# Attention steps taken in pairs in a two-stage vision block on one Trainium2 core

## The chip, the core and the metric

The kernel runs on one core of a Trainium2 chip. The metric is the device time of one execution in microseconds; for the kernel before it is 3094.75 us, the median of three runs. Times in the text are microseconds unless marked ns.

## What is computed

For each of 4 images of 32 x 32 tokens with 384 channels a selective scan comes first and attention second, both with a residual. The change touches the attention alone. Cut to that:

```python
qkv = (x.reshape(B, L, dim) @ w_qkv + b_qkv).reshape(B, L, 3, nh, hd)   # L = 1024, nh = 12, hd = 32
...
q = rot(q)
k = rot(k)
attn = jnp.einsum('bnqd,bnkd->bnqk', q, k) * scale
...
attn = attn.reshape(B, nh, H, W, H, W) + rel_h[..., :, None] + rel_w[..., None, :]
attn = jax.nn.softmax(attn.reshape(B, nh, L, L), axis=-1)
out = jnp.einsum('bnqk,bnkd->bnqd', attn, v)
out = out.transpose(0, 2, 1, 3).reshape(B, H, W, dim)
return out @ w_proj + b_proj
```

## The kernel before

The scan stage takes the first 1.7 ms and is not touched. Then each image has its attention by itself, some 347 us each. An image begins with a start phase (projections of q and k, values, relative-position tables; `START`) and then runs 96 steps: 3 groups of 4 heads (`GROUPS`, `HG`), 8 blocks of 128 queries in a group (`QB`), one head in a step. In step s = 32 g + k, the block is k // 4 and the head k % 4.

A step has these parts. TensorE's `scores(s)` (L880) multiplies one block's queries by all 1024 keys: two products of 64 rows of the array, one in its upper and one in its lower half, with the relative bias folded in as further rows. VectorE's `biased_scores(s)` (L1201) adds the bias of the other axis, writes the result to a buffer `PR` in SBUF and takes the negated maximum. ScalarE (L1526) takes the exponential in place and the row sum. TensorE's `turn_probs(s)` (L891) transposes the 128 x 1024 probabilities in eight pieces of the full array. `save_turned(s)` copies them from PSUM to `PT`: VectorE (L1155) for even s, ScalarE (L1503) for odd s. After a block's four steps, `weigh` (L905) multiplies by the values, 64 products of 32 columns of the array each, in two halves of 32; ScalarE's `save_sums` (L1509) copies the result.

PSUM has eight banks. A step's scores and its transposes take two banks each out of banks 0 to 5, so three places turn; bank 6 holds the weighing, bank 7 the jobs. Jobs are work of the next group that is put between the steps: a projection in two steps of a group (`proj`, six matmuls, L561; ScalarE's copy L1495; VectorE's two products L1125 and L1126; GpSimd's sum L1636) and the relative tables (`rel` L854 and L1141, `relh` L843 and L1146), at the steps of `JOB_AT`. Each job's output has bank 7, so its matmuls wait until the job before was copied out. In the last group `LATE` puts the sums' transposes (L925), the normalisation (L934, then L1171 and L1172 on VectorE) and half of the output projection (L561, L1179) in the same way; each waits for the one before.

The order is that of the loops in each engine's program. TensorE issues `scores(s + 2)`, then the job, then half a weighing in every second step, then `turn_probs(s)`. At a change of group SyncE loads 4 heads' operands with 6 DMAs each (L542), as soon as the last scores of the old group with that head are done, that is after step 28 + j of the group for head j; `scores` of the first four steps of a group wait for them. An image ends with `invert_sums(2)` (L1189), the last sums' transposes, weighing 23 and the rest of the projection (L948). The next image's start phase follows at once.

## Time and profile before

| | |
|---|---|
| median of 3 runs | 3094.75 us (3092.77 to 3095.74) |
| profiled execution | 3094.16 us, span 3092.4 us |
| busy share of the span | TensorE 87%, VectorE 73%, ScalarE 52%, GpSimd 44% |
| first scores of images 0 to 3, from the span's start | 1737.13, 2083.66, 2429.98, 2777.37 us |
| mean granted TensorE clock | 0.968 of full; 1.00 in the attention after its first start phase |

The profile has a timeline of each engine (start and duration, and in brackets how long the engine had been idle and what released it), groups of instructions by line, and windows with the busy time of each engine in a stretch. The ends of matmuls are modelled, and neighbours overlap: the time that a block of matmuls takes from the engine is read from its start to the start of the next block. The first and the last attention image of the trace run alike, so that image 1 stands for all four here.

### The profile page before, as it was taken

The page shows a single profiled execution, that of the slowest core. Times are in us where ns is not written, and L with a number is a line of the kernel's source. Part 1 is how long each engine was busy: PE and PEld are TensorE (multiplying, and loading weights), DVE is VectorE, ACT ScalarE, POOL GpSimd, SP SyncE. Part 2 cuts the span into 40 slices and gives each one's busy share as a digit, 9 for nine tenths or more (in the row PEclk, how much of TensorE's full clock was granted, in tenths as well). Part 3 has the DMA queues.
Part 4 walks back from the last instruction along what each step waited for, and adds up shares of the span by engine and source line. Part 5 has one row for each costly group of instructions (what it writes and reads, how often), then busy time and mean ns, then how long its engine had stood idle before and what let it go on. Part 6 is the DMA issues. An engine that isn't in the chain of part 4 may idle for free. (4 is left out here: it accounts for less than half of the span.)

```text
span 3092.4 us, 40835 instructions
## 1 busy us (share of the span) xinstructions
PE 2684.6 (87%) x16088; PEld 1346.6 (44%) x16088; DVE 2242.5 (73%) x2157; ACT 1614.7 (52%) x1972; POOL 1351.2 (44%) x624
## 2 busy tenths in 40 slices
PE   5579788988889878687767999999999999999999
PEld 2134233333333333232322565555555565556555
DVE  0398988899888998899992566646665566646665
ACT  2464655555555556555541456625564356525564
POOL 1577887887778877788670200011000300011000
PEclk9799999999999999999996999999999999999999
DMA  2344544455444555445551210120120210120110
GB/s 78 108 142 129 163 150 144 150 140 168 165 145 148 142 170 167 154 160 140 197 172 36 76 36 18 39 75 1 36 56 14 63 36 22 35 76 1 35 36 22
DMA packets 93526, 297.03 MB, mean 96 GB/s; under 512 B 16172, under 2 KB 18872, under 8 KB 93208
## 3 DMA queue, kind: packets, MB, share of 16 engines
q1 hardware_dynamic: 93336, 294.43, 30.8%
q8 instruction: 128, 2.10, 0.3%
q14 instruction: 62, 0.51, 0.1%
HBM read 238.27 MB, written 23.07 MB: 85 GB/s over the span
## 5 line engine op out<-in xcount | busy, mean ns | idle before, releaser
L1599 POOL TENSOR_TENSOR arena<-arena 128x1024 f32<-128x1024 f32 x384 | 903.2, 2357 | 307.4 <-DVE arena L1081 297.7
L1081 DVE TENSOR_TENSOR_SCAN arena<-PS,arena 128x1024 f32<-128x1024 f32 x384 | 879.0, 2289 | 102.2 <-ACT PS L1442 70.9
L577 PE MATMUL PS<-arena,ident 128*128 128x512 f32 x1536 | 762.0, 620 | 15.0 <-ACT arena L1453 12.8
L1442 ACT ACTIVATE PS<-arena,a_inf,a_neg 128x1024 f32<-128x1024 f32 x384 | 463.8, 1208 | 586.3 <-DVE arena L1081 580.3
L1201 DVE CUSTOM_DVE_ANT_1 arena<-PS,arena 128x1024 f32<-128x1024 f32 x384 | 467.7, 1219 | 323.4 <-PE PS L880 321.8
L1526 ACT ACTIVATE arena<-arena,neg_max 128x1024 f32<-128x1024 f32 x384 | 441.0, 1148 | 494.8 <-DVE neg_max L1201 494.8
L1089 DVE TENSOR_TENSOR arena<-arena,PS 128x1024 f32<-128x1024 f32 x384 | 460.8, 1200 | 57.7 <-PE PS L568 56.4
L568 PE MATMUL PS<-arena,sel 96*128 96x512 bf16 x768 | 239.4, 394 | 295.5 <-DVE arena L1089 291.7
L1629 POOL TENSOR_TENSOR arena<-arena 128x512 f32<-128x512 f32 x48 | 68.4, 1425 | 955.2 <-ACT arena L1495 955.2
L880 PE MATMUL PS<-arena 64*128 64x512 f32 x1536 | 431.6, 640 | 19.3 <-DMA arena<-arena 12.8
L577 PEld LDWEIGHTS PS<-arena,ident 128*128 128x128 f32 x1536 | 302.5, 198 | 275.0 <-issue 221.4
L891 PE MATMUL PS<-ident,arena 128*128 128x128 f32 x3072 | 414.7, 278 | 3.8 <-ACT arena L1526 3.6
L891 PEld LDWEIGHTS PS<-ident,arena 128*128 128x128 f32 x3072 | 334.9, 142 | 154.9 <-issue 92.5
L568 PEld LDWEIGHTS PS<-arena,sel 96*128 96x128 bf16 x768 | 55.9, 100 | 577.5 <-DVE arena L1089 503.3
L1155 DVE COPY arena<-PS 128x1024 f32<-128x1024 f32 x192 | 233.9, 1218 | 60.6 <-PE PS L891 57.2
L905 PEld LDWEIGHTS PS<-arena 128*32 128x32 f32 x6144 | 157.0, 110 | 134.0 <-issue 131.7
L905 PE MATMUL PS<-arena 128*32 128x128 f32 x6144 | 206.5, 276 | 0.0
L1503 ACT ACTIVATE arena<-PS 128x1024 f32<-128x1024 f32 x192 | 192.7, 1004 | 19.4 <-PE PS L891 19.4
L880 PEld LDWEIGHTS PS<-arena 64*128 64x128 f32 x1536 | 116.5, 185 | 88.5 <-issue 59.0
L1636 POOL TENSOR_TENSOR arena<-arena 128x512 f32<-128x512 f32 x48 | 64.0, 1333 | 176.3 <-DVE arena L1126 175.7
L561 PE MATMUL PS<-normed,arena 128*128 128x512 f32 x288 | 135.7, 615 | 0.6 <-DVE g_tmp L1025 0.6
L577 PE MATMUL PS<-arena 128*128 128x512 f32 (+1 forms) x224 | 108.3, 622 | 12.0 <-ACT arena L1305 5.5
(125 smaller groups left out, 2205.3 us busy)
## 6 DMA issues: line engine op xcount, KB each, us to landing
arena<-b_rows SPq DMA_DIRECT2D x256, 512.0 KB, 3.7
arena<-b_rows SPq DMA_DIRECT2D x256, 256.0 KB, 3.9
arena<-arena SPq DMA_DIRECT2D x192, 128.0 KB, 3.3
arena<-arena SPq DMA_DIRECT2D x120, 64.0 KB, 2.6
normed<-x_in SPq DMA_DIRECT2D x12, 512.0 KB, 5.4
residual<-x_in SPq DMA_DIRECT2D x12, 512.0 KB, 5.6
x<-residual SPq DMA_DIRECT2D x12, 512.0 KB, 5.3
xn<-residual SPq DMA_DIRECT2D x12, 512.0 KB, 4.7
```

What stands on the lines that cost most here:

```text
L568: last = pe.matmul(dst[:, half(h)], lhs, rhs(h), start=(k == 0), stop=(k == len(pairs) - 1))
L577: last = pe.matmul(dst[:, half(h)], lhs, rhs[:, half(h)], start=start, stop=stop, skip_group_check=True)
L880: last = pe.matmul(scores_place(s)[:, h * HALF:(h + 1) * HALF], QX[rows, j, qb * P:(qb + 1) * P], KX[rows, j, :], start=True, stop=True)
L891: last = pe.transpose(turned_place(s)[:, t * P:(t + 1) * P], PR[s % 3][:, t * P:(t + 1) * P], idn)
L905: last = pe.matmul(banks(6, 1)[HD * j:HD * j + HD, (n % 2) * P:(n % 2 + 1) * P], V[:, t, head * HD:(head + 1) * HD], PT[:, n % 2, j, t, :] ...
L1081: dve.tensor_tensor_scan(HS[:, at % 2, ::step], DA[:, ::step], DBU[:, at % R3, ::step], 0.0, ALU.mult, ALU.add).then_inc(scan_done.sem, 1)
L1089: dve.tensor_tensor(HC[:, at % R_HC, :], HS[:, at % 2, :], C_PSUM, ALU.mult).then_inc(hc_ready.sem, 1)
L1155: dve.tensor_copy(PT[:, n % 2, s % HG, :, :], turned_place(s).rearrange("p (t q) -> p t q", t=QB)).then_inc(pt_saved[0].sem, 1)
L1201: dve.tensor_tensor_reduce(out=PR[s % 3].rearrange("p (h w) -> p h w", w=IMG), in0=scores_place(s).rearrange("p (h w) -> p h w", w=IMG), i ...
L1442: act.activation(DA, DELTA[:, tile % 2, :], ACT.Exp, bias=a_inf[:, col:col + 1], scale=a_neg[:, col:col + 1]).then_inc(da_ready.sem, 1)
L1526: act.activation(PR[s % 3], PR[s % 3], ACT.Exp, bias=neg_max[:, s % 4:s % 4 + 1], scale=-1.0, accum_out=row_sum[:, qb, at:at + 1]).then_in ...
L1599: pool.tensor_tensor(DBU[:, at % R3, :], DU[:, tile % 2, :], BSB[:, at % R3, :], ALU.mult).then_inc(dbu_ready.sem, 1)
```

## The change

Steps go in pairs (s even, s + 1). TensorE issues `scores(s + 2)` and `scores(s + 3)`, the pair's job, a whole weighing of 64 products when s is a multiple of 4, then `turn_probs(s)` and `turn_probs(s + 1)`. A fourth `PR` buffer lies in `group_mean`, which is not used in this stage. The scores of a step and its transposes now have the same place (`step_place`), and a place is shared by steps 1 and 2, 3 and 4 and so on. So `scores(s + 2)` waits until VectorE has read step s + 1 (`max_done`), and `turn_probs(s + 1)` until it has read step s + 2. VectorE takes both steps of a pair, then copies the odd step's transposes out, then does its share of the jobs; ScalarE copies the even step's. The jobs of group 0 stand at steps 2, 4, ..., 28.

```diff
-        PR = [from_mats(k)[:, 0, :] for k in (6, 7, 26)]
+        PR = [from_mats(k)[:, 0, :] for k in (6, 7, 26)] + [
+            W["group_mean"][:, :, :].rearrange("p k c -> p (k c)")[:, 0:L]]
...
-        def step_banks(n):
-            return banks((0, 4, 2)[n % 3])
-        def scores_place(s):
-            return step_banks(s if s < 3 else 2 * s - 2)
-        def turned_place(s):
-            return step_banks(2 * s + 3)
+        def step_place(s):
+            return banks((4, 0, 2)[(s + 1) // 2 % 3])
...
-        JOB_AT = [{k: m for m, k in enumerate([2, 4, 6, 8, 10, 12, 16, 18, 20, 22, 24, 25, 26, 27])}, {6: 0, 10: 1}, {}]
+        JOB_AT = [{2 + 2 * m: m for m in range(len(JOBS[1]))}, {6: 0, 10: 1}, {}]
...
-                    if s == 1:
+                    if s == 0:
                         pe.wait_ge(rel_saved.sem, rel_saved.after(b, 2))
-                    elif s == 3:
-                        pe.wait_ge(max_done.sem, max_done.after(b, 2))
-                    elif s >= 4:
-                        wait_turned_saved(s - 4)
+                    elif s % 2 == 0:
+                        pe.wait_ge(max_done.sem, max_done.after(b, s))
+                    elif s >= 5:
+                        wait_turned_saved(s - 5)
                     for h in range(2):
                         rows = slice(2 * HD * h, 2 * HD * h + 2 * HD)
-                        last = pe.matmul(scores_place(s)[:, h * HALF:(h + 1) * HALF],
+                        last = pe.matmul(step_place(s)[:, h * HALF:(h + 1) * HALF],
                                          QX[rows, j, qb * P:(qb + 1) * P], KX[rows, j, :], start=True, stop=True)
                     last.then_inc(s_psum.sem, 1)
                 def turn_probs(s):
                     pe.wait_ge(exp_done.sem, exp_done.after(b, s + 1))
-                    if s + 1 < STEPS * GROUPS:
+                    if s % 2 and s + 1 < STEPS * GROUPS:
                         pe.wait_ge(max_done.sem, max_done.after(b, s + 2))
-                    else:
-                        wait_turned_saved(s - 3)
+                    elif s % 2 == 0 and s:
+                        wait_turned_saved(s - 1)
                     for t in range(QB):
-                        last = pe.transpose(turned_place(s)[:, t * P:(t + 1) * P], PR[s % 3][:, t * P:(t + 1) * P], idn)
+                        last = pe.transpose(step_place(s)[:, t * P:(t + 1) * P], PR[s % 4][:, t * P:(t + 1) * P], idn)
                     last.then_inc(pt_psum.sem, 1)
...
                 scores(0)
                 scores(1)
-                for s in range(STEPS * GROUPS):
+                for s in range(0, STEPS * GROUPS, 2):
                     g, k = divmod(s, STEPS)
                     if s + 2 < STEPS * GROUPS:
                         scores(s + 2)
-                    if k in JOB_AT[g]:
-                        job(g + 1, JOB_AT[g][k])
-                    if g + 1 == GROUPS and k in LATE_AT:
-                        late(LATE_AT[k])
-                    if s % 2 == 1 and s > HG:
-                        weigh((s - HG - 1) // HG, (s - HG - 1) % HG // 2)
-                    if s + 1 == STEPS * GROUPS:
+                        scores(s + 3)
+                    for k in (k, k + 1):
+                        if k in JOB_AT[g]:
+                            job(g + 1, JOB_AT[g][k])
+                        if g + 1 == GROUPS and k in LATE_AT:
+                            late(LATE_AT[k])
+                    if s % HG == 0 and s:
+                        weigh(s // HG - 1, 0, 1)
+                    if s + 2 == STEPS * GROUPS:
                         wait_turned_saved(s - 2)
                         project(0, (0, 1))
                         project(1, (0, 1))
                     turn_probs(s)
+                    turn_probs(s + 1)
...
-                    dve.tensor_copy(PT[:, n % 2, s % HG, :, :], turned_place(s).rearrange("p (t q) -> p t q", t=QB)
-                                    ).then_inc(pt_saved[0].sem, 1)
+                    dve.tensor_copy(PT[:, n % 2, s % HG, :, :], step_place(s).rearrange("p (t q) -> p t q", t=QB)
+                                    ).then_inc(pt_saved[1].sem, 1)
...
-                    if s >= 3:
-                        dve.wait_ge(pt_psum.sem, pt_psum.after(b, s - 2))
+                    if s >= 4:
+                        dve.wait_ge(pt_psum.sem, pt_psum.after(b, s - 3))
                     bias = RELH[g][:, (qb * HG + j) * IMG:(qb * HG + j + 1) * IMG]
                     dve.tensor_tensor_reduce(
-                        out=PR[s % 3].rearrange("p (h w) -> p h w", w=IMG),
-                        in0=scores_place(s).rearrange("p (h w) -> p h w", w=IMG),
+                        out=PR[s % 4].rearrange("p (h w) -> p h w", w=IMG),
+                        in0=step_place(s).rearrange("p (h w) -> p h w", w=IMG),
...
                     job(0, m)
-                for s in range(STEPS * GROUPS):
+                for s in range(0, STEPS * GROUPS, 2):
                     g, k = divmod(s, STEPS)
-                    if s % 2 == 1 and s > 2:
-                        save_turned(s - 3)
                     biased_scores(s)
-                    for after, kinds in ((4, ("proj",)), (2, ("rel", "relh"))):
-                        if k - after in JOB_AT[g] and JOBS[g + 1][JOB_AT[g][k - after]][0] in kinds:
-                            job(g + 1, JOB_AT[g][k - after])
-                    if g + 1 == GROUPS and k - 2 in LATE_AT:
-                        late(LATE_AT[k - 2])
-                    if g + 1 == GROUPS:
-                        if k == 2:
-                            invert_sums(0)
-                        elif k == STEPS // 2 + 2:
-                            invert_sums(1)
+                    biased_scores(s + 1)
+                    if s:
+                        save_turned(s - 1)
+                    for k in (k, k + 1):
...
-                save_turned(STEPS * GROUPS - 2)
+                save_turned(STEPS * GROUPS - 1)
                 invert_sums(2)
...
-                    if s % 2 == 0 and s > 3:
-                        save_turned(s - 3)
-                    if s % HG == 2 and s > 2 * HG:
-                        save_sums(s // HG - 2)
+                    if s % 2 == 0 and s:
+                        save_turned(s - 2)
+                    if s % HG == 2 and s > HG:
+                        save_sums(s // HG - 1)
                     act.wait_ge(max_done.sem, max_done.after(b, s + 1))
                     at = HG * g + j
-                    act.activation(PR[s % 3], PR[s % 3], ACT.Exp, bias=neg_max[:, s % 4:s % 4 + 1], scale=-1.0,
+                    act.activation(PR[s % 4], PR[s % 4], ACT.Exp, bias=neg_max[:, s % 4:s % 4 + 1], scale=-1.0,
...
-                save_turned(STEPS * GROUPS - 3)
-                save_sums(QB * GROUPS - 2)
-                save_turned(STEPS * GROUPS - 1)
+                save_turned(STEPS * GROUPS - 2)
                 save_sums(QB * GROUPS - 1)
```

In the middle of a group without jobs, TensorE's program reads before (scores L880, weighing L905, transposes L891):

```order
L880 MATMUL PS<-arena 128x512 [waits pt_saved_1]
L880 MATMUL PS<-arena 128x512
L905 MATMUL PS<-arena 32x128 x16
L891 MATMUL PS<-ident,arena 128x128 [waits max_done,exp_done]
L891 MATMUL PS<-ident,arena 128x128 x7
L880 MATMUL PS<-arena 128x512 [waits pt_saved_0]
L880 MATMUL PS<-arena 128x512
L891 MATMUL PS<-ident,arena 128x128 [waits max_done,exp_done]
L891 MATMUL PS<-ident,arena 128x128 x7
L880 MATMUL PS<-arena 128x512 [waits pt_saved_1]
L880 MATMUL PS<-arena 128x512
```

and now (scores L876, transposes L887, weighing L901):

```order
L887 MATMUL PS<-ident,arena 128x128 [waits pt_saved_1,exp_done]
L887 MATMUL PS<-ident,arena 128x128 x7
L887 MATMUL PS<-ident,group_mean 128x128 [waits max_done,exp_done]
L887 MATMUL PS<-ident,group_mean 128x128 x7
L876 MATMUL PS<-arena 128x512 [waits max_done]
L876 MATMUL PS<-arena 128x512
L876 MATMUL PS<-arena 128x512 [waits pt_saved_0]
L876 MATMUL PS<-arena 128x512
L901 MATMUL PS<-arena 32x128 [waits o_saved,pt_saved_1,pt_saved_0]
L901 MATMUL PS<-arena 32x128 x31
L887 MATMUL PS<-ident,arena 128x128 [waits pt_saved_1,exp_done]
L887 MATMUL PS<-ident,arena 128x128 x7
```

The two steps' scores stand side by side, the weighing is whole, and the first scores of a pair wait for VectorE's `max_done` where all had waited for a copy out of PSUM.

On VectorE, at a normalisation in the last group, before (L1171 and L1172 the normalisation, L1155 the copy, ISA the biased scores):

```order
L1171 TENSOR_TENSOR arena<-arena,PS 128x512 [waits o_saved,rb_psum]
L1172 TENSOR_SCALAR arena<-arena,b_qkv 128x512 [waits dve_step]
L1155 COPY arena<-PS 128x1024 [waits o_psum,pt_psum]
L1201 ISA arena,neg_max<-PS,arena 128x1024 [waits pt_psum,s_psum]
L1201 ISA neg_max 128x1
L1201 ISA arena,neg_max<-PS,arena 128x1024 [waits pt_psum,s_psum]
L1201 ISA neg_max 128x1
```

and now:

```order
L1154 COPY arena<-PS 128x1024 [waits o_psum,pt_psum]
L1170 TENSOR_TENSOR arena<-arena,PS 128x512 [waits o_saved,rb_psum]
L1171 TENSOR_SCALAR arena<-arena,b_qkv 128x512 [waits dve_step]
L1200 ISA arena,neg_max<-PS,arena 128x1024 [waits pt_psum,s_psum]
L1200 ISA neg_max 128x1
L1200 ISA group_mean,neg_max<-PS,arena 128x1024 [waits pt_psum,s_psum]
L1200 ISA neg_max 128x1
```

The normalisation stands behind the copy of the transposes instead of ahead of it, and both steps' scores stand behind it.

At the end of an image TensorE has before (L948 the output projection, L925 the sums' transposes):

```order
L891 MATMUL PS<-ident,arena 128x128 x7
L905 MATMUL PS<-arena 32x128 x16
L948 MATMUL PS<-arena 128x512 [waits pt_saved_1]
L948 MATMUL PS<-arena 128x512 x3
L891 MATMUL PS<-ident,arena 128x128 [waits pt_saved_0,exp_done]
L891 MATMUL PS<-ident,arena 128x128 x7
L925 MATMUL PS<-ident,arena 4x128 [waits pj_read,rs_ready]
L925 MATMUL PS<-ident,arena 4x128 x3
```

and now (L944, L921):

```order
L944 MATMUL PS<-arena 128x512 [waits pt_saved_0]
L944 MATMUL PS<-arena 128x512 x3
L887 MATMUL PS<-ident,arena 128x128 [waits pt_saved_1,exp_done]
L887 MATMUL PS<-ident,arena 128x128 x7
L887 MATMUL PS<-ident,group_mean 128x128 [waits exp_done]
L887 MATMUL PS<-ident,group_mean 128x128 x7
L921 MATMUL PS<-ident,arena 4x128 [waits pj_read,rs_ready]
L921 MATMUL PS<-ident,arena 4x128 x3
```

There VectorE has before, and now:

```order
L1155 COPY arena<-PS 128x1024 [waits o_psum,pt_psum]
L1201 ISA arena,neg_max<-PS,arena 128x1024 [waits pt_psum,s_psum]
L1201 ISA neg_max 128x1
L1155 COPY arena<-PS 128x1024 [waits o_psum,pt_psum]
L1189 RECIPROCAL arena<-arena 128x4x4 [waits exp_done]
L1166 COPY arena<-PS 4x512 [waits rt_psum]
```

```order
L1154 COPY arena<-PS 128x1024 [waits o_psum,pt_psum]
L1178 SCALAR_TENSOR_TENSOR arena<-PS,b_proj,residual 128x512 [waits pj_psum]
L1154 COPY arena<-PS 128x1024 [waits o_psum,pt_psum]
L1188 RECIPROCAL arena<-arena 128x4x4 [waits exp_done]
L1165 COPY arena<-PS 4x512 [waits rt_psum]
```

Two transposes instead of one stand ahead of the sums', and the copy that VectorE makes ahead of the reciprocal is that of the last step, no longer that of the last but one.

## Rows read from the trace of the kernel before

**Rows 1.** Windows: stretch, its length, busy time (and instructions) by engine, clock.

```profile
2083.00:2394.00 311.00, 303.68 (x2993) 180.13 (x2993) 199.98 (x292) 172.50 (x273) 20.13 (x16) 1.00 0.11 27
```

**Rows 2.** Timeline of TensorE in group 1: start, duration, engine, line.

```profile
2250.16 1.13 PE L880 MATMUL PS<-arena 64*128 64x512 f32 x4
2251.22 1.08 PE L905 MATMUL PS<-arena 128*32 128x128 f32 x32
2252.23 1.09 PE L891 MATMUL PS<-ident,arena 128*128 128x128 f32 x8
2253.25 1.13 PE L880 MATMUL PS<-arena 64*128 64x512 f32 x4
```

**Rows 3.** Timeline of TensorE at the first steps of image 1.

```profile
2083.66 2.85 PE L880 MATMUL PS<-arena 64*128 64x512 f32 x12 [0.58 <-ACT arena L1483]
2087.40 1.09 PE L891 MATMUL PS<-ident,arena 128*128 128x128 f32 x8 [0.89 <-ACT arena L1526]
```

**Rows 4.** Timeline of TensorE at the end of image 1.

```profile
2377.34 1.97 PE L891 MATMUL PS<-ident,arena 128*128 128x128 f32 x16
...
2387.96 1.96 PE L905 MATMUL PS<-arena 128*32 128x128 f32 x64
```

**Rows 5.** Timeline of VectorE in image 1, at three places.

```profile
2085.99 1.22 DVE L1201 CUSTOM_DVE_ANT_1 arena<-PS,arena 128x1024 f32<-128x1024 f32 x1
...
2087.13 1.22 DVE L1201 CUSTOM_DVE_ANT_1 arena<-PS,arena 128x1024 f32<-128x1024 f32 x1
...
2299.52 0.68 DVE L1171 TENSOR_TENSOR arena<-arena,PS 128x512 f32<-128x512 f32 x1
2300.24 0.49 DVE L1172 TENSOR_SCALAR arena<-arena,b_qkv 128x512 f32<-128x512 f32 x1
2300.64 1.22 DVE L1155 COPY arena<-PS 128x1024 f32<-128x1024 f32 x1
...
2380.49 0.24 DVE L1189 RECIPROCAL arena<-arena 128x16 f32<-128x16 f32 x1
```

**Rows 6.** Timeline of all engines where transposes wait for VectorE.

```profile
2237.49 0.08 DVE L1201 DVE_READ_ACCUMULATOR2_ANT neg_max<- 128x1 f32 x1
...
2237.72 1.06 PE L891 MATMUL PS<-ident,arena 128*128 128x128 f32 x8
...
2238.75 1.00 ACT L1503 ACTIVATE arena<-PS 128x1024 f32<-128x1024 f32 x1
```

**Rows 7.** Groups of instructions by line, steps of image 1: busy, mean ns, idle.

```profile
L1126 DVE TENSOR_TENSOR arena<-arena 64x512 f32<-64x512 f32 x8 | 5.5, 684 | 0.1
...
L1141 DVE COPY arena<-PS 128x256 f32<-128x256 f32 x8 | 3.0, 420 | 2.9 <-PE PS L854 2.9
L1495 ACT ACTIVATE arena<-PS,b_qkv 128x512 f32<-128x512 f32 x4 | 2.7, 687 | 1.0 <-PE PS L561 1.0
```

**Rows 8.** Timeline of TensorE at both changes of group, image 1.

```profile
2176.54 1.13 PE L880 MATMUL PS<-arena 64*128 64x512 f32 x4
...
2197.13 1.13 PE L880 MATMUL PS<-arena 64*128 64x512 f32 x4 [1.03 <-DMA arena<-arena]
...
2268.78 1.13 PE L880 MATMUL PS<-arena 64*128 64x512 f32 x4
...
2288.55 1.13 PE L880 MATMUL PS<-arena 64*128 64x512 f32 x4 [0.80 <-DMA arena<-arena]
```

**Rows 9.** Timeline of SyncE's DMA queue at the first of them.

```profile
2177.77 16.00 SPq L542 DMA_DIRECT2D arena<-arena  x24
```

**Rows 10.** Timeline of TensorE in the scan stage, around an idle stretch.

```profile
907.44 1.88 PE L577 MATMUL PS<-arena,ident 128*128 128x512 f32 x4
911.76 0.61 PE L568 MATMUL PS<-arena,sel 96*128 96x512 bf16 x2 [2.44 <-DVE arena L1089]
912.21 3.50 PE L577 MATMUL PS<-arena,ident 128*128 128x512 f32 x4
```

**Rows 11.** Windows behind that stretch, columns as in rows 1.

```profile
912.30:915.70 3.40, 3.40 (x6) 1.34 (x5) 3.24 (x3) 3.06 (x4) 2.19 (x2) 0.50 0.43 130
```

More of the change, by code:

```diff
@@ L1502, in save_turned @@
                         act.wait_ge(o_psum.sem, o_psum.after(b, n - 1))
-                    act.activation(PT[:, n % 2, s % HG, :, :], turned_place(s).rearrange("p (t q) -> p t q", t=QB),
-                                   ACT.Copy).then_inc(pt_saved[1].sem, 1)
+                    act.activation(PT[:, n % 2, s % HG, :, :], step_place(s).rearrange("p (t q) -> p t q", t=QB),
+                                   ACT.Copy).then_inc(pt_saved[0].sem, 1)
                 def save_sums(n):
```

10 lines of the change are left out of this document (added).

## The prediction, made before the changed kernel was run

> **What bounds the kernel now.** I read the windows first. In the stretch of one image's 96 steps TensorE is busy for 303.7 of 311 us at full clock, VectorE for 200, ScalarE for 173 [rows 1]. Then TensorE's timeline: its blocks follow each other with no idle time but for a handful of waits, so that an image costs what its blocks cost. A block costs the time to the next block's start: scores 1.06, half a weighing 1.01, transposes 1.02 [rows 2]. These contain more than the products. Three steps' scores in a row take 2.85 with the tail of the last [rows 3], against 1.13 for one alone [rows 2]: each further one costs 0.86. A second block of transposes behind the first adds 1.97 - 1.09 = 0.88 by duration [rows 2, 4], 0.87 by their starts, and a second half weighing 1.96 - 1.08 = 0.88 likewise, 0.87 by starts. So each change from one kind of block to another costs 0.12 to 0.20, and the change removes some of these. The rest of the argument is on what it adds.
>
> **Savings on TensorE.** Four steps without jobs cost before 4 x 1.06 + 4 x 1.02 + 2 x 1.01 = 10.35. In pairs they cost 2 x (1.06 + 0.86) + 2 x (1.02 + 0.87) + (1.01 + 0.87) = 9.51: 0.84 less, 0.21 a step. An image has 24 such fours: 20.2. Off go 0.55 for the blocks that stand side by side before already (three scores at the start, two transposes at the end), 0.15 for the last weighing, whole before, and 1.25 for jobs: nine full-array jobs stand ahead of a whole weighing now, where before each ran into the transposes, and pay one more change, some 0.15 (the 1.02 against 0.87 above). 18.3 an image is left, 73 in all.
>
> **The new loop through VectorE** [rows 5, 6]. Call 0 the start of scores(s + 2). TensorE has the next pair ready at 3.81 (1.92 + 1.89). VectorE can copy out step s - 1 from 0.11; two of its large instructions start 1.145 apart (2085.99 to 2087.13), so it reads step s + 2 from 1.25 and step s + 3 from 2.40, and is done at 2.40 + 1.15 + 0.08 = 3.63. The transposes at 2237.72 started 0.15 after the end of such a reading, so scores(s + 4) can start at 3.78. That is 0.03 before TensorE gets there: without jobs the loop costs nothing, but whatever VectorE has to do in such a pair beyond this, D, delays TensorE by D - 0.03. ScalarE's copy (1.00), then two exponentials of 1.15, end at 2.6 to 2.8, ahead of the second transposes at 2.85: nothing.
>
> **Waits that come in, an image.**
> Start: scores(2) waits for the reading of step 1, which ends at 1.18 + 1.145 + 1.23 = 3.55, and starts at 3.7 instead of 1.82: 1.8. Before, the first transposes waited 0.9 [rows 3]. Net 0.9.
> Jobs of group 0: a job starts at 1.92 if the output before it is out. VectorE's share stands behind the copy, so it starts at 1.25. A `rel` copy (2 x 0.42) ends at 2.0, a `relh` copy (0.68) at 1.9, which costs with 0.1 for the signal 0.2 three times and 0.1 twice; at step 16 the two products of a projection (2 x 0.69) stand ahead of the `rel` copy: 1.6; ScalarE's projection copy (0.69) behind its exponential ends at 2.0 or 2.15: 0.13 or 0.28, six times [rows 7]. In sum 3.6.
> Group 1, step 14: the two products in a pair with neither job nor weighing cost 1.4; a wait of 1.2 stands there before. Net 0.2.
> Normalisation, group 2: one takes 0.72 + 0.49 = 1.21 [rows 5], ends at 2.46, and the next late job starts at 2.56 instead of 1.92: 0.64 four times; shorter ones 0.1 to 0.2, five times; where no job follows, D is 1.12 once and 0.2 once. In sum 4.6.
> End: the last copy of VectorE now is step 95's; it starts 0.2 after TensorE's last transposes, the reciprocal 1.15 later, takes 0.24 [rows 5], and only then the sums' transposes can start: 1.7. The projection ahead waits 0.4 for ScalarE's copy of step 92. Queued behind both is all that ends the image, the next image's start phase included. In sum 2.1.
>
> **The DMA stretches.** From scores(28) to scores(35) 20.6 us pass, from scores(60) to scores(67) 19.8 [rows 8]. In both the last start is the landing of the 24th DMA; SyncE's queue needs 16 us for the 24 issues, starting when scores(28) are done [rows 9]. Nothing in the change makes these earlier. TensorE's own work there was 19.5 and 17.6 and becomes 16.3 and 14.3. So these 14 steps save nothing: the waits grow from 3.3 to 9.8, net 6.5.
>
> **The sum.** 0.9 + 3.6 + 0.2 + 4.6 + 2.1 + 6.5 = 17.9 us of new waits against 18.3 saved: 0.4 an image, some 2 in all (term by term by the segments of the steps I get 2.7; I take 2.5). From the profiled execution's 3094.2 this gives 3091.7; it lies 0.6 under the median, so 3092.3 on the median's scale.
>
> **The clock.** The stall at scores(35) has one piece of 3.3 us idle, where now it is 1.0; at scores(67) two pieces of some 2 us, or one of 2.7. In the scan stage an idle stretch of 2.44 us [rows 10] was followed by a window at 0.50 [rows 11], that is 1.2 instead of 2.4 GHz. Of 19 idle stretches of 2.4 to 3.5 us there, 15 were followed by such a fall of mostly 3.4 us, of 9 of 1.65 to 1.8 us three; in the attention none, at waits of up to 1.7. What one costs: four matmuls that take 1.88 at full clock took 3.50 [rows 10], so 3.4 us at the low level lose about 1.6. The work behind the stall is TensorE's alone, so it is lost in full. Eight stalls give about six falls: 9.5 us. **3092.3 + 9.5 = 3101.8.**
> The Trainium skill bears on this (TensorE: Matmul & The Clock Gate, "Why this matters for your kernels"): it warns of idle gaps between bursts, since after one the clock falls to half; by the length it gives, most of my eight would be too short, two or three falls were left and the time would be 3097. The trace has falls after shorter ones, so I go by the trace.
>
> **Rivals.**
> (a) The stalls don't bring the clock down, since they fall apart into shorter waits on heads 1, 2 and 3. The attention has no fall in the trace now; against it stand 15 of 19. Then 3092, within 0.2%.
> (b) The waits behind VectorE don't arise, because jobs' copies and normalisations are short against what TensorE has queued. They are 8.4 an image; without them and with the falls 3068, with half of them 3085. Against it: each is a position in the program, worked out from durations that vary by 1%.
> (c) Slower: VectorE becomes the bound. It decides at 0.03 us of margin: if copies, readings and signals take 0.3 more in a pair, the seven unburdened pairs of an image and the five waits that are already VectorE's grow by it: 12 x 0.3 x 4 = 14, 3116. For it: three engines touch PSUM in a tighter order. Against: readings next to each other at 1.145 are in the trace while TensorE writes.
> The Trainium skill has this as a rule (TensorEngine Tiling (Array Packing), "PSUM Bottleneck"): speeding up TensorE by tiles leaves the copies out of PSUM as the next bound. Here its sum would be (c)'s; the trace puts it just short.
> (d) That adjacent blocks don't merge their cost is excluded by rows 3 and 4.
>
> **How the numbers follow.** Forecast 0.47, (a) 0.23, (b) 0.14, (c) 0.16. The forecast's own range, with 4 to 8 falls and 1 us an image of error in the waits, is 3095 to 3109. A measurement of this kernel tells about 0.2% (6 us) from no change: slower is over 3101, faster under 3088.6. The forecast lies across 3101, with 0.3 of its 0.47 above it; with (c) slower is 0.45. Same: the rest of it and (a), 0.38. Faster: (b) and the low edge of (a), 0.17. The range, 3083 to 3114, leaves out most of (b) and the far part of (c).
>
> **What would show it.** In the changed profile: sixteen transposes and eight scores as single blocks of 1.9; scores(35) and scores(67) 20 to 21 us after scores(28) and scores(60), with idle stretches of 2.4 to 3.3 us; windows behind them at 0.50, the mean clock lower than 0.968; 0.6 ahead of L930 and L557 in group 2; 1.5 idle ahead of L921 at the end. Wrong would be: pairs without job or weighing well over 3.8 (c), no falls (a), or scores(28) to scores(35) under 20 us, which would free 6 us an image.

## The result, and the profile after

The changed kernel takes 3106.39 us in the median of 6 runs (3103.94 to 3110.08), the kernel before beside it 3094.6 (3092.77 to 3095.74). The ratio is 1.0040, with a 95% interval of 1.0028 to 1.0052: slower by 12 us. The forecast was 3101.8, its range 3083 to 3114, and slower had the largest chance. The profiled execution took 3105.91 us with a span of 3104.0; its mean granted clock is 0.962, where before it was 0.968.

The first view is the windows, as in [rows 1]: the stretch of image 1's steps to behind the last wait of the image, then a piece of it. The columns are the stretch, its length, busy time of TensorE, its weight loads, VectorE, ScalarE and GpSimd, the clock, the DMA engines' share and GB/s.

```profile
2087.17:2398.60 311.43, 291.75 (x2990) 187.93 (x2991) 197.69 (x291) 166.38 (x272) 20.16 (x16) 0.98 0.09 26
...
2290.00:2295.60 5.60, 5.60 (x69) 3.49 (x70) 1.23 (x2) 0.00 (x0) 0.00 (x0) 0.52 0.58 233
```

TensorE is busy for 291.75 us of 311, where it was 303.68: the products and their changes did get cheaper, by 12 us in this window. But the stretch is no shorter: from scores(0) to the last part of the output projection (L944, L948 before) 309.94 us pass, where it was 307.96. And its clock is 0.98 and no longer 1.00, with a piece at 0.52. The timeline of TensorE in group 1 shows the blocks, as [rows 2] does before:

```profile
2239.88 1.99 PE L876 MATMUL PS<-arena 64*128 64x512 f32 x8
2241.80 1.09 PE L887 MATMUL PS<-ident,arena 128*128 128x128 f32 x8
2244.04 1.07 PE L887 MATMUL PS<-ident,group_mean 128*128 128x128 f32 x8 [1.15 <-DVE neg_max L1200]
2245.10 1.99 PE L876 MATMUL PS<-arena 64*128 64x512 f32 x8
2247.01 1.96 PE L901 MATMUL PS<-arena 128*32 128x128 f32 x64
2248.90 1.97 PE L887 MATMUL PS<-ident,arena 128*128 128x128 f32 x16
2250.80 1.56 PE L876 MATMUL PS<-arena 64*128 64x512 f32 x6
```

Two scores take 1.92 from start to start, a whole weighing 1.89, two transposes 1.90, as forecast. The wait of 1.15 inside a pair of transposes is one where VectorE had both products of a projection to do. Three more stretches of TensorE's timeline, in the order of time: the start of the image ([rows 3]), step 16, and the change from group 1 to group 2 ([rows 8]).

```profile
2087.17 1.99 PE L876 MATMUL PS<-arena 64*128 64x512 f32 x8 [0.58 <-ACT arena L1484]
2090.87 1.99 PE L876 MATMUL PS<-arena 64*128 64x512 f32 x8 [1.71 <-DVE neg_max L1200]
...
2146.14 1.99 PE L876 MATMUL PS<-arena 64*128 64x512 f32 x8
2149.72 2.04 PE L850 MATMUL PS<-arena 128*128 128x64 f32 x16 [1.60 <-DVE arena L1140]
2151.70 3.35 PE L901 MATMUL PS<-arena 128*32 128x128 f32 x64
...
2289.90 2.08 PE L876 MATMUL PS<-arena 64*128 64x512 f32 x4 [2.76 <-DMA arena<-arena]
2291.91 3.64 PE L901 MATMUL PS<-arena 128*32 128x128 f32 x64
```

A weighing that takes 1.96 at full clock takes 3.35 behind the idle 1.60 of step 16, and 3.64 behind the idle 2.76 of the group's change: the clock has fallen to its lower level (0.52 granted in the window from 2290.00 above). SyncE's queue, which needed 16.00 in [rows 9], issues the 24 loads of the first change in 15.41 here:

```profile
2183.49 15.41 SPq L538 DMA_DIRECT2D arena<-arena  x24
```

The longest of TensorE's waits in the attention, by releaser, in us, times and the longest one. They are counted from 1750 us on, so without the first steps of image 0, and shorter ones follow in the view:

```profile
PE PS L876 <- DMA arena<-arena: 30.5, 17, 2.8
PE PS L887 <- DVE neg_max L1200: 8.0, 10, 1.1
PE PS L944 <- DVE arena L1171: 6.8, 4, 1.7
PE PS L850 <- DVE arena L1140: 6.4, 4, 1.6
PE PS L921 <- DVE arena L1188: 5.9, 4, 1.5
PE PS L876 <- DVE neg_max L1200: 5.1, 3, 1.7
PE PS L930 <- DVE arena L1171: 4.9, 8, 0.6
```

The same view of the kernel before has two of them:

```profile
PE PS L880 <- DMA arena<-arena: 12.8, 12, 1.7
PE PS L948 <- DVE arena L1172: 6.8, 4, 1.7
```

So the 6.8 ahead of L944 (L948 before) is unchanged, the waits for the heads' loads have more than doubled, and the others are new. The table has the time between scores, read from their starts, for images 0 to 3, and the forecast, which counted the falls of the clock apart. Of its last column 20.6 and 19.8 stand in the prediction. The other four do not, they are a division of its terms among the segments; all six together give the 2.7 us that it names for the whole program.

| from, to | before | after | forecast without falls |
|---|---|---|---|
| scores(0), (28) | 92.88 each | 93.46, 95.08, 95.07, 95.03 | 93.65 |
| (28), (35) | 20.76, 20.59, 21.30, 20.39 | 19.60, 19.00, 20.03, 20.54 | 20.6 |
| (35), (60) | 71.65 each | 70.18, 68.56, 70.17, 70.18 | 68.41 |
| (60), (67) | 19.81, 19.77, 20.13, 19.45 | 20.34, 20.08, 20.32, 19.29 | 19.8 |
| (67), (95) | 86.73 each | 85.35, 85.31, 82.67, 85.56 | 83.07 |
| (95), next (0) | 54.71 | 60.26 | 60.16 |

Where a segment has two values, the granted clock tells them apart: 70.18 has a fall of 3.4 us, 68.56 none; 85.3 to 85.6 have one of 6.8 us, 82.67 none; 95.03 to 95.08 one of 3.4 us, 93.46 none. There are ten falls in the attention, 44 us at the lower level, and none before, if the one in the last 5 us of either is left out.

### The profile page after: what moved, and what is told of

The parts are those of the page before. It is cut to its first block and busy times, and to the rows that moved or that the text cites. A ratio compares the mean times of both kernels' runs of the same rounds, so it can differ in the third digit from the quotient of the medians.

```text
span 3104.0 us, 40819 instructions
## 1 busy us (share of the span) xinstructions
PE 2640.9 (85%) x16088; PEld 1378.6 (44%) x16088; DVE 2236.2 (72%) x2157; ACT 1592.3 (51%) x1972; POOL 1351.9 (44%) x624
## 5 line engine op out<-in xcount | busy, mean ns | idle before, releaser
L876 PE MATMUL PS<-arena 64*128 64x512 f32 x1536 | 390.3, 624 | 39.8 <-DMA arena<-arena 30.5
L1200 DVE CUSTOM_DVE_ANT_1 arena<-PS,arena 128x1024 f32<-128x1024 f32 x288 | 343.2, 1215 | 37.1 <-PE PS L876 36.2
L1527 ACT ACTIVATE arena<-arena,neg_max 128x1024 f32<-128x1024 f32 x288 | 328.7, 1143 | 10.0 <-DVE neg_max L1200 10.0
L887 PE MATMUL PS<-ident,arena 128*128 128x128 f32 x2304 | 293.1, 277 | 0.0
L887 PEld LDWEIGHTS PS<-ident,arena 128*128 128x128 f32 x2304 | 252.7, 142 | 75.9 <-issue 42.4
L876 PEld LDWEIGHTS PS<-arena 64*128 64x128 f32 x1536 | 132.2, 187 | 172.2 <-issue 79.9
L901 PEld LDWEIGHTS PS<-arena 128*32 128x32 f32 x6144 | 172.9, 115 | 62.2 <-issue 59.9
L901 PE MATMUL PS<-arena 128*32 128x128 f32 x6144 | 200.4, 286 | 0.0
L1200 DVE CUSTOM_DVE_ANT_1 group_mean<-PS,arena 128x1024 f32<-128x1024 f32 x96 | 117.1, 1219 | 22.9 <-PE PS L876 22.9
```

The costliest lines, as they stand in the source:

```text
L876: last = pe.matmul(step_place(s)[:, h * HALF:(h + 1) * HALF], QX[rows, j, qb * P:(qb + 1) * P], KX[rows, j, :], start=True, stop=True)
L887: last = pe.transpose(step_place(s)[:, t * P:(t + 1) * P], PR[s % 4][:, t * P:(t + 1) * P], idn)
L901: last = pe.matmul(banks(6, 1)[HD * j:HD * j + HD, (n % 2) * P:(n % 2 + 1) * P], V[:, t, head * HD:(head + 1) * HD], PT[:, n % 2, j, t, :] ...
L1200: dve.tensor_tensor_reduce(out=PR[s % 4].rearrange("p (h w) -> p h w", w=IMG), in0=step_place(s).rearrange("p (h w) -> p h w", w=IMG), in1 ...
L1527: act.activation(PR[s % 4], PR[s % 4], ACT.Exp, bias=neg_max[:, s % 4:s % 4 + 1], scale=-1.0, accum_out=row_sum[:, qb, at:at + 1]).then_in ...
```

## The experiments

All times are medians. "Before" is the kernel before in the same session; the last column is the difference to the kernel after by the ratios, which leaves the sessions' own difference out.

| kernel | us | before | ratio, 95% interval | against after, us |
|---|---|---|---|---|
| e1_fill | 3095.72 | 3093.84 | 1.0009 (1.0000 to 1.0018) | -10 |
| e2_jobs_first | 3066.00 | 3093.84 | 0.9913 (0.9899 to 0.9926) | -39 |
| e3_recip_first | 3097.63 | 3093.84 | 1.0010 (1.0001 to 1.0019) | -9 |
| e4_two_queues | 3105.49 | 3093.84 | 1.0034 (1.0021 to 1.0047) | -2 |
| e5_front | 3055.17 | 3092.71 | 0.9878 (0.9863 to 0.9893) | -50 |
| e11_front_one_queue | 3089.55 | 3093.52 | 0.9987 (0.9977 to 0.9996) | -16 |
| e6_before_front | 3080.15 | 3092.71 | 0.9956 (0.9939 to 0.9973) | |
| e7_whole_weigh | 3107.02 | 3092.71 | 1.0047 (1.0032 to 1.0062) | |
| e8_all | 3011.29 | 3092.71 | 0.9736 (0.9722 to 0.9751) | -94 |
| e9_dve_in_loop | 3013.78 | 3092.75 | 0.9744 (0.9730 to 0.9759) | |
| e10_dve_in_gap | 3011.21 | 3092.75 | 0.9740 (0.9724 to 0.9757) | |

The theory was that of the prediction: the pairs save what they should, and it is lost again to waits for the heads' loads, to waits behind VectorE's copy and to the clock that falls behind such waits. The rivals were that the falls or the waits cost little, or that VectorE as a whole is the bound.

### Does the clock cost what it seems to? (e1_fill)

```diff
+                        fill(s, 0)
                         scores(s + 2)
+                        fill(s, 1)
                         scores(s + 3)
...
+                def fill(s, odd):
+                    n = {(STEPS, 1): 4, (2 * STEPS, 0): 2, (2 * STEPS, 1): 2}.get((s, odd), 0)
...
+                    for _ in range(n):
+                        pe.matmul(banks(7, 1), idn, W["w_qkv"][:, 0, 0:HALF], start=True, stop=True,
+                                  skip_group_check=True)
```

> The kernel after, with eight extra matmuls (128x512, into bank 7, read by nobody, so the output is what it was) per image in TensorE's waits for the heads' DMAs: four ahead of scores(35), two ahead of scores(66), two ahead of scores(67). They take about 0.43 us each (six of this shape take 2.6), less than the waits that stand there (2.0 to 2.7, and 1.5 to 2.8), so by themselves they delay nothing. The trace of after shows seven falls of the clock behind these waits, 34 us at half speed in all. Theory A (falls come from these idle stretches and cost 1.6 us per 3.4 us): the seven vanish, the time goes down by 11 to 16 us, to about 3092, and the mean granted clock rises by 0.005. Rival B (the low clock in the rows costs little, since the loop waits for VectorE or the DMAs anyhow): within 3 us of after. Rival C (the falls do not depend on idle time here): falls remain and the time stays at 3106.

Measured: 10 us faster than after, mean clock 0.967. The expectation had the length of the extra matmuls wrong by half. They take 0.91 each, as TensorE's timeline ahead of scores(35) shows, and so delayed the scores:

```profile
2198.70 1.13 PE L876 MATMUL PS<-arena 64*128 64x512 f32 x4
2199.76 3.70 PE L949 MATMUL PS<-arena,ident 128*128 128x512 f32 x8
2203.39 1.13 PE L876 MATMUL PS<-arena 64*128 64x512 f32 x4
```

Scores(28) to (35) grew by 4.3 us over the four images, (60) to (67) by 0.7. Of the seven falls behind changes of group one was left, in image 0, inside (60) to (67), which took 21.67 there and 19.59 to 19.86 in the other images. Yet the program is faster, since (35) to (60) is 68.56 and (67) to (95) is 82.67 in all four images: TensorE did useless work, late, and the useful work behind it ran at full clock. Theory A holds, but for the one fall that stayed. That a fall behind the change of group costs 1.6 (3.4 us long) or 2.6 to 2.9 (6.8 us long) is shown, not only read off: 3 x 1.6 + 3 x 2.7 = 13 us. With the 5.0 lost in the stretches, and 1.6 less behind step 16 in this execution, that is 9.7, against the 10 measured. The seventh fall, in image 2, lies between two waits inside (60) to (67), which took 20.32 with it and 19.29 to 20.34 in the other images: there a landing set the end, and no cost can be seen.

### Do the jobs wait because of their place? (e2_jobs_first)

```diff
                     biased_scores(s + 1)
-                    if s:
-                        save_turned(s - 1)
                     for k in (k, k + 1):
...
                                 invert_sums(1)
+                    if s:
+                        save_turned(s - 1)
```

> The kernel after, with VectorE's shares of jobs and late work placed ahead of its copy of the odd step's transposes in each pair. Theory A (jobs wait because their share stands behind a copy of 1.15): the idle time ahead of L850, L557, L930 and ahead of the sums' transposes, some 16 us in the trace of after, goes; so do the three falls behind step 16, 5 us: 15 to 21 us faster, 3086 to 3091. Rival B (VectorE is the bound in these pairs, so the order of its work does not matter): 0 to 5 us faster. Rival C (the copy, now later by up to 1.4, holds up the next transposes): slower, 3110.

Measured: 39 us faster than after, twice what was expected. VectorE's timeline of this kernel at step 16 of image 1, and TensorE's:

```profile
2135.31 0.69 DVE L1124 TENSOR_TENSOR arena<-arena 64x512 f32<-64x512 f32 x1
2136.01 0.68 DVE L1125 TENSOR_TENSOR arena<-arena 64x512 f32<-64x512 f32 x1
2136.73 0.76 DVE L1140 COPY arena<-PS 128x256 f32<-128x256 f32 x2
2137.67 1.23 DVE L1154 COPY arena<-PS 128x1024 f32<-128x1024 f32 x1 [0.19 <-PE PS L887]
...
2137.57 1.99 PE L876 MATMUL PS<-arena 64*128 64x512 f32 x8
2139.48 2.04 PE L850 MATMUL PS<-arena 128*128 128x64 f32 x16
```

The three jobs' shares run while VectorE would wait for TensorE's transposes in any case (it is idle for 0.19 still), the copy starts where it did, 0.10 behind the scores, and the 1.60 ahead of L850 is gone. Two terms had been left out of the expectation. The 8.0 us ahead of L887 went as well: those pairs had a normalisation or two products behind the copy and ahead of the next reading, which now lie in the gap. And falls in group 2 were not counted: (67) to (95) has one in a single image now, 80.40 against 78.8 in the others, where after had a long one in three. Without falls (0) to (28) is 2.1 shorter and (67) to (95) 3.9 in each image, 24 us. In (35) to (60) the wait behind two products (1.4 us in the pair of scores(48)) is gone as well, 6 us in all: e8 below, which has no fall there, takes 67.06 against 68.56. By the segments the falls cost 7.5 us less here than in the kernel after, and what is left of the 39 is a little at the image's end and in the stretches.

### The end of an image (e3_recip_first)

```diff
-                save_turned(STEPS * GROUPS - 1)
                 invert_sums(2)
+                save_turned(STEPS * GROUPS - 1)
```

> The kernel after, with the reciprocal of the last sums placed ahead of VectorE's copy of step 95. Theory A (the end of an image waits for that copy): the 1.48 us idle ahead of L921 goes in each image, and the copy itself has room, since the projection stands between it and the last weighing: 4 x 1.5 = 6 us faster, 3100.5. Rival B (something later sets the end of an image): no difference.

Measured: 9 us faster than after, with single runs from 3091.5 to 3102.7. The profile gives the part that is this edit's: scores(95) to the next image's scores(0) went from 60.26 to 58.69, 4 x 1.57 = 6.3 us. The other 3 us are open. Fewer or shorter falls in other executions would fit the spread of single runs, but the profiled execution (3101.52) does not show it: it has eight falls where after's has ten, four of them long, and by the segments they cost 17.8 us against 17.9.

### What sets the landing of the heads? (e4, e5, e11, e6)

The prediction put the 24th landing down to SyncE's issues. In e4 GpSimd's queue loads heads 1 and 3:

```diff
+        SP_HEADS, POOL_HEADS = (0, 2), (1, 3)
...
+        def load_heads(eng, b, g, heads):
+            ...
+            for j in heads:
+                eng.wait_ge(s_psum.sem, s_psum.after(b, STEPS * g - HG + j + 1))
+                for dst, src in operands(g, j):
+                    eng.dma_start(dst, src).then_inc(loads(j, g + 1)[0].sem, 16)
```

> The kernel after, with heads 1 and 3 of groups 1 and 2 loaded by GpSimd's own DMA queue and heads 0 and 2 by SyncE's. Theory A (24 issues of 0.67 us one behind the other on SyncE's queue set the end of the two stretches): scores(28) to scores(35) fall from 19.8 to 16.5 us and scores(60) to scores(67) from 20.0 to about 15, and the falls behind them go: 4 x (3.3 + 5) = 33 and 11 us, to between 3062 and 3075. Rival B (the DMA engines or the bytes set it, or GpSimd's issues take as long as two of SyncE's): the stretches stay at 19 to 20 us and the time within 5 us of 3106, or longer if GpSimd's work on q and k comes late.

Measured: the same as after. All issues were out 10 us after scores(28), and the last landed at 19.3 to 20.1 nevertheless in seven of the eight changes (18.3 in one), where the kernel after has 19.0 to 20.5. SyncE's own last load of the first change was issued at 9.1 in images 0 and 1 and landed at 19.1 and 19.5, ten us later; in the kernel after the last load lands some 3 us behind its issue. The stretches themselves became longer, 20.3 and 21.4 in the mean against 19.8 and 20.0: with the heads' loads mixed, head 2 is late too, and scores(34) and (66) start at 18.3 to 19.8 and no longer at 15.9 to 17.0. The time is the same in spite of that, since 6 us less pass in the other segments and the scan stage took 1.8 less in this execution. A window of 15 us inside the first change of group of image 1, of this kernel and then of the kernel after, has the DMA engines' share and rate in its last columns:

```profile
2185.00:2200.00 15.00, 11.94 (x155) 8.20 (x153) 9.83 (x15) 10.00 (x16) 5.20 (x10) 1.00 1.00 153
```

```profile
2185.00:2200.00 15.00, 13.95 (x176) 9.46 (x168) 11.41 (x18) 9.89 (x16) 0.00 (x0) 1.00 0.59 167
```

With two queues the engines are busy all the time (1.00, after 0.59) and move no more. This is rival B: with two queues the bytes set the landing. The Trainium skill has the rule (DMA: Bandwidth & Descriptors, "Issuing engines are not separate DMA queues"): all issuing engines feed the same DMA engines, and a second one only saves time on the sequencer, which it calls usually small. The first half agrees with this run (153 and 167 GB/s). The second does not agree with e5 and e11 below, where the issues take about as long as the bytes.

So e5 asks for fewer bytes ahead of the first scores. A block of scores needs all of k, but only 128 columns of q and of the table:

```diff
+            for first in (True, False):
+                for j in range(HG):
+                    ...
+                    at = slice(0, FRONT) if first else slice(FRONT, L)        # FRONT = 256
...
+                    if qb == FRONT // P:
+                        for loaded, count in rests(j, g + 1):
+                            pe.wait_ge(loaded.sem, loaded.after(b, count))
```

> The kernel after, with the heads' loads of groups 1 and 2 in two parts. First, for all four heads, both halves of k and the first 256 columns of q and of the relative table (256 of 640 KB a head), then the rest, which scores wait for two blocks later; SyncE's queue and GpSimd's share the issues. With two queues alone all issues were out 10 us after scores(28) and the last landing still came at 19.5 to 20.1. Theory A (the bytes moved, at 130 to 140 GB/s, set the landing): the first parts are 1 MB, 7 to 8 us, so head 3 can start 10 to 13 us after scores(28), and the stretches fall to TensorE's own work: scores(28) to scores(35) from 19.8 to 16.3 to 17, scores(60) to scores(67) from 20.0 to 14.3 to 15, 34 us in all, and with the waits the seven falls of the clock go, 11 to 14 us: 3106 - 34 - 12 = 3060. Rival B (each DMA costs a time of its own, in issue or landing, so that more of them are no quicker): the stretches stay over 19, 3100 to 3110.

Measured: 50 us faster than after, and all four images alike: scores(28) to (35) 16.83, (60) to (67) 14.29, against 16.3 and 14.3 of TensorE's own work. No wait for a DMA is left, and of the falls only two behind step 16. The rest of the q and table columns lands at 20.3, when nobody waits for it yet. e11 issues the same two parts on SyncE's queue alone:

> The kernel after, with the loads in two parts as before, but all issued on SyncE's queue. Two queues alone gave nothing, two queues with two parts 51 us. Theory A (both limits are close: the bytes, at 140 GB/s, and SyncE's issues, one in 0.62 to 0.67 us): the 24 first issues still end 16 us after they start, 17 after scores(28), and the last lands some 2 us behind: scores(28) to scores(35) 18.3 to 18.8 us instead of 19.8 in the mean, scores(60) to scores(67) the same instead of 20.0; waits shrink by 2.5 us an image and some falls go: 3106 - 10 - 3 = 3093, with 3085 to 3098 for the falls. Rival B (the bytes alone set the landing): 3055 as with two queues.

Measured: 16 us faster than after, with (28) to (35) at 17.83 to 18.64 and (60) to (67) at 18.11 to 19.26. Its queue in image 1, and the two queues of e5 at the same place:

```profile
2174.47 26.17 SPq L430 DMA_DIRECT2D arena<-arena  x40
```

```profile
2169.56 13.62 SPq L433 DMA_DIRECT2D arena<-arena  x20
...
2170.05 3.30 POOL L433 DMA_DIRECT2D arena<-arena  x6 [33.73 <-PE PS L911]
2174.66 7.46 POOL L433 DMA_DIRECT2D arena<-arena  x14 [1.31 <-PE PS L911]
```

In e11 the issues do set it: the 24th starts at 15.9 and lands at 17.8 (over all changes 15.9 to 17.0 and 17.8 to 19.2). In the kernel after, the 24th starts at 16.1 to 17.3 and lands 2.9 to 3.4 later. So two limits lie close together: with one queue the issues, and the last landing behind them, end 19.9 us behind scores(28) or (60) in the mean (the kernel after), with two queues the bytes end at 19.6 (e4). Taking away the issues alone gave 2 us (e4), the bytes alone 16 us (e11: in its profile 11 in the stretches and 8 from cheaper falls), both 50, falls included. The same edit on the kernel before:

> The kernel before, with the same loads in two parts over two queues. TensorE's own work in the stretches is 19.5 and 17.6 us there, against 20.8 and 19.8 that pass. Theory A: they fall to about 19.5 and 17.6: 4 x (1.3 + 2.2) = 14 us faster, 3080. So the loads cost the kernel before 14 us and the kernel after some 45. Rival B: no difference.

Measured: 3080.15 against 3092.71, 12.6 us faster, with (28) to (35) at 19.49 and (60) to (67) at 17.61 in all images, TensorE's own work as the prediction gave it (19.5 and 17.6). The loads cost the kernel before 13 us and the kernel after 50, with the falls behind them.

### A whole weighing alone (e7_whole_weigh)

```diff
-                    if s % 2 == 1 and s > HG:
-                        weigh((s - HG - 1) // HG, (s - HG - 1) % HG // 2)
+                    if s % HG == 1 and s > HG:
+                        weigh((s - HG - 1) // HG, 0, 1)
```

> The kernel before, with a block's weighing whole in every fourth step in place of halves in every second, and nothing else of the change. Theory A (a block change costs 0.12 to 0.15 of TensorE, and one weighing block fewer in each of 23 fours of an image saves one or two): 23 x 0.14 x 4 = 13 us faster or some more, 3081. Rival B (a whole weighing delays the next transposes and scores by a further 0.87, VectorE and ScalarE run dry behind it and TensorE waits): 0 to +20.

Measured: 14 us slower than before. TensorE's waits in the attention, and the timelines of TensorE and ScalarE at a place in group 1:

```profile
PE PS L880 <- ACT arena L1503: 20.4, 40, 0.6
```

```profile
2209.49 1.13 PE L880 MATMUL PS<-arena 64*128 64x512 f32 x4 [0.60 <-ACT arena L1503]
2210.55 1.95 PE L905 MATMUL PS<-arena 128*32 128x128 f32 x64
...
2207.28 1.15 ACT L1526 ACTIVATE arena<-arena,neg_max 128x1024 f32<-128x1024 f32 x1 [1.03 <-DVE neg_max L1201]
...
2208.43 1.00 ACT L1503 ACTIVATE arena<-PS 128x1024 f32<-128x1024 f32 x1
```

The weighing costs one block less, as said (1.88, not 2 x 1.01; 3.1 us less an image in the profile of image 1, 12.5 in all), but TensorE idles for 6 us more in that image. In front of a weighing three steps now follow each other in 2.08 each, and ScalarE's copy (2208.43) stands behind an exponential that waited 1.03 for VectorE, so the scores wait 0.60 for the copy. Halves in every second step gave ScalarE its time. So this part of the change pays only together with the pairs, where scores wait for a reading and not for that copy.

### Is VectorE the bound? (e8, e9, e10)

> The kernel after with three of the edits together: VectorE's jobs ahead of its copy (40 us alone), the reciprocal ahead of the last copy (8 us alone), loads in two parts. Theory A (separate waits, so they add up; the falls of the clock are shared, some 10 us counted twice): 3106 - 40 - 7 - 34 - 5 = 3020. Rival B (the stretches are held up by the landings in any case): 3058.

e8 puts e2, e3 and e5 together: 3011.29, 81 us faster than before and 94 than after. The parts alone add up to 39 + 9 + 50 = 98. The 4 us that are missing fit falls counted twice: they cost 17.9 in the kernel after, and e2 alone has 7.5 less of it, e5 alone 14.6. All of TensorE's waits in its attention, again from 1750 us on:

```profile
PE PS L979 <- DVE arena L1206: 6.8, 4, 1.7
PE PS L911 <- DVE neg_max L1235: 5.1, 3, 1.7
PE PS L911 <- ACT arena L1519: 1.7, 3, 0.6
PE PS L588 <- ACT arena L1531: 1.6, 8, 0.2
PE PS L979 <- ACT arena L1539: 1.0, 4, 0.2
PE PS L881 <- ACT arena L1531: 0.8, 4, 0.2
```

On it two small copies were added to each pair, on VectorE's way from the copy to the next reading (e9) or in its gap (e10):

```diff
+                        for i in range(2):
+                            at = 64 * (s % 4 + i)
+                            dve.tensor_copy(W["last_taps"][:, 0, at:at + 64], W["cos"][:, 0, 0:64])
```

> The fastest kernel so far (3011.3 us: jobs ahead of the copy, the reciprocal ahead of the last copy, loads in two parts) with two small copies of 64 columns on VectorE in each pair, behind the copy of the odd step and ahead of the next reading, into columns that nobody reads. Theory A (the loop through VectorE ends 0.03 ahead of TensorE in a pair without weighing or job, as the prediction has it): if the two copies move the next reading by x, each such pair, some 8 to 9 an image, grows by x - 0.03. By the neighbours (a reciprocal of 16 columns 0.24, a readout 0.08) x is 0.2 to 0.4: 9 x 4 x 0.17 to 0.37 = 6 to 13 us slower. Rival B (there is more room than 0.03): within 2 us of 3011.

> The same two small copies, but behind the two readings of the pair and ahead of the copy of the odd step, where VectorE waits for TensorE's transposes. Theory A (what VectorE does in that gap is free until it fills it, which is why the jobs cost nothing there and up to their whole length behind the copy): the gap is 0.3 to 0.9 us in a short pair, so 0 to 2 us slower than 3011. Rival B (VectorE's busy time per pair counts, wherever it stands): as slow as with the copies in the loop, 6 to 13 us.

Measured: e9 +2.5, with intervals of both that overlap, and e10 0. The profile tells more than the medians. A pair without weighing or job, VectorE's and then TensorE's timeline of e9:

```profile
2219.48 1.22 DVE L1189 COPY arena<-PS 128x1024 f32<-128x1024 f32 x1 [2.04 <-PE PS L922]
2220.62 0.28 DVE L1263 COPY last_taps<-arena 128x64 f32<-128x64 f32 x2
2220.82 1.22 DVE L1235 CUSTOM_DVE_ANT_1 arena<-PS,arena 128x1024 f32<-128x1024 f32 x1
...
2223.11 0.08 DVE L1235 DVE_READ_ACCUMULATOR2_ANT neg_max<- 128x1 f32 x1
...
2219.37 1.99 PE L911 MATMUL PS<-arena 64*128 64x512 f32 x8
...
2223.25 1.99 PE L911 MATMUL PS<-arena 64*128 64x512 f32 x8
```

The reading starts 1.34 behind the copy, where it was 1.14: x is 0.20. The pair takes 3.87 from start to start where it took 3.81, seven such pairs an image, and two at the changes of group grow by 0.16. So the loop through VectorE without the addition takes 3.87 - 0.20 = 3.67, and the margin is 0.14, not 0.03. In e10 every pair is what it was. The rule of theory A is right, its margin was not.

## Why the prediction was right, and where it was not

**Savings on TensorE: right.** The blocks take 1.92, 1.89 and 1.90, and 18.3 an image was forecast. The cleanest comparison is e8 with e6_before_front, neither of which waits for loads: (28) to (60) takes 83.23 against 91.14, (60) to (67) 14.29 against 17.61, (67) to (95) 78.7 against 86.72. Over an image it is 17 us, with the waits that are left in e8 still in it.

**Start, end and jobs: right to some tenths.** The waits stand at the places named: 1.71 ahead of scores(2) (1.8 forecast), 1.60 at step 16 (1.6), 0.6 ahead of L930, 1.48 ahead of L921 (1.5). Scores(95) to the next image took 60.26, where the table's last column has 60.16. With the projection's products in group 1 a pair takes 5.22 (2239.88 to 2245.10 above), 1.4 more than the 3.81 of one without (1.4).

**The loop through VectorE: right in kind, its margin mis-sized.** 0.03 was forecast, 0.14 is measured (e9). The sum took the 0.15 between the end of a readout and TensorE's start from one place [rows 6]; in e9 the readout ends at 2223.19 and the scores start at 2223.25, so that 0.06 is enough. With it the sum gives 3.69, near the 3.67 measured. It moved little, since in the pairs that matter VectorE is late by 0.3 to 1.2.

**The DMA stretches: the size right, the cause half of it.** 20.6 and 19.8 were forecast, 19.8 and 20.0 are the means after. That they would save next to nothing was so. The step that named SyncE's 24 issues as what sets the end describes the kernel after: its 24th load is issued at 16.1 to 17.3 and lands some 3 us later. But it had nothing to say of the bytes, and with the issues out at 10 us the landing stayed (e4). Issues and bytes are limits of nearly the same length. Also (28) to (35) did shrink by 1.0 an image, and lies under 20 us in two of four images, which the prediction had named as a sign of being wrong. What moved the landings forward there is open; part of it may be scatter, since e3, whose loads are the same, has a mean of 20.1.

**The clock: the step that failed by size.** Six falls of 1.6 were forecast, 9.5 us. There were seven behind the changes of group, and they cost 13 us, since three are 6.8 us long and not 3.4; three more came behind step 16, 3 x 1.6 = 4.8, at a wait of 1.60 that the prediction had in its list at the right length but held to be too short. 18 us in all. The trace of the kernel before left this more open than the prediction's three of nine says: in the scan stage only three idle stretches lie between 1.6 and 1.85 us (1.79, 1.80, 1.79), and a fall follows each of them, but none follows the four of 1.56 to 1.58. The others of the nine lie in the attention. Against the falls, the waits came out 4.4 us shorter than forecast over the program, three of them in the DMA stretches. 3104.0 - 3092.4 = 11.6 us of span are 17.9 of falls, 7.1 saved between the scores, and 0.9 that the scan stage took longer in this execution.

**The rivals.** (a), no falls: excluded, and e1 shows their price. (b), waits behind VectorE do not arise: excluded, e2 and e3 came out 39 and 9 us faster by removing them, falls included. (c), VectorE as the bound: excluded as put. The Trainium skill's warning that the copies out of PSUM may become the next bound (TensorEngine Tiling (Array Packing), "PSUM Bottleneck") is borne out only in part: in the pairs without other work VectorE is done 0.14 us ahead of TensorE, and what cost time was not how much it did but in which order (e2, e10).

The result thus lies 4.6 us over the forecast: falls 8.4 more, waits 4.4 less, and 0.6 that is no more than the 0.9 of the stage before. That it lies so close is in part luck: two errors of opposite sign.

## What to carry to other kernels

A rearrangement that saves the busiest engine time is worth what the waits around it leave: here 68 to 73 us were saved and all lost, and three small edits off TensorE brought 94 back. Put an engine's side work where it waits for the bottleneck anyway, ahead of the instruction whose input comes last, and load first what the first block needs. If a transfer sets a time, vary its issue and its bytes apart: two limits of nearly the same length hide each other, and removing one gives only the distance to the other.

## What the runs showed of the hardware

**Falls after a short wait.** In the six kernels that have the wait of 1.60 at step 16 (after, e1, e3, e4, e5, e11) the clock fell behind 11 of its 24 occurrences, never in image 0. In the same kernels none fell behind the 1.71 ahead of scores(2), the 1.48 (where it exists) and the 1.71 at an image's end. The 1.60 is followed by sixteen products of 64 columns (L850), the wait ahead of scores(2) by scores of 512. The Trainium skill (TensorE: Matmul & The Clock Gate, "Why this matters for your kernels") warns of longer idle gaps between bursts than these; here gaps of 1.6 to 2.8 were enough, so the measurement decides. What tells the 11 from the 13 is not settled.

**A fall costs half its length or less.** One of 3.4 us cost 1.62, one of 6.8 us 3.18 at step 16 (in e1 and e3, 96.64 against 93.46) and 2.6 to 2.9 in group 2, where TensorE has further waits for VectorE that a slower TensorE may have covered.

**DMA engines' share.** Between SBUF and SBUF, 32 partitions a transfer, a share of 1.00 moved 153 GB/s and one of 0.59 moved 167 (e4 and after). With two queues the share is no measure of what is moved. An issue took GpSimd's queue 0.55 (3.30 for six, e5) and SyncE's 0.64 (15.41 for 24, after).
